# Filling matmuls between early pairs of first looks, and the grouped attention's first scores ahead of its last four value blocks

## The reference

```python
q = jnp.einsum('bsh,he->bse', x, w_q).reshape(b, sq, GROUPS, HPG, KVC)
k, v = jnp.split(jnp.einsum('bsh,he->bse', x, w_kv), 2, axis=-1)
scores = jnp.where(causal, jnp.einsum('bqgpd,bkgd->bgqpk', q, k) * SCALE, -jnp.inf)
ctx = jnp.einsum('bgqpk,bkgd->bqgpd', softmax(scores), v)
out = jnp.einsum('bse,eh->bsh', ctx, w_dense)
```

## Time and the profile before

| | us |
|---|---|
| median of three runs | 1053.94 |
| lowest, highest run | 1052.57, 1057.13 |
| the profiled execution | 1061.46 |
| its span in the trace | 1059.4 |
| TensorE busy in it | 972.7 (92%) |
| VectorE busy | 745.6 (70%) |
| ScalarE busy | 572.0 (54%) |
| GpSimd busy | 394.4 (37%) |

### The profile page before, as it was taken

The page is one execution under the profiler, slowest core; times in us unless marked ns, Lnnn a source line. Parts: engine busy times, 40 slices in busy tenths (PEclk is TensorE's granted clock), DMA queues, the critical chain, the costliest instruction groups (busy, mean ns, idle before and its releaser), DMA issues.

```text
span 1059.4 us, 20929 instructions
## 1 busy us (share of the span) xinstructions
PE 972.7 (92%) x7863; PEld 668.7 (63%) x7888; DVE 745.6 (70%) x1867; ACT 572.0 (54%) x1166; POOL 394.4 (37%) x259
## 2 busy tenths in 40 slices
PE   4999789999999999999988879999999999999897
PEld 3787633433443344688777657777777777777776
DVE  7856966888888883454666756777776777777655
ACT  6443413566666667544454545565655555565354
POOL 3010130045324540000244046565656555566254
PEclk9999978999999999999989999999999999999999
DMA  4020543255423502021010000000000000000001
GB/s 110 1 83 2 164 85 60 55 90 97 88 61 76 98 22 72 1 88 73 1 41 1 0 2 1 2 2 2 2 2 2 2 1 2 1 1 2 1 1 41
DMA packets 25373, 37.93 MB, mean 36 GB/s; under 512 B 3096, under 2 KB 21192, under 8 KB 23752
## 3 DMA queue, kind: packets, MB, share of 16 engines
q1 hardware_dynamic: 25272, 36.59, 14.6%
HBM read 30.53 MB, written 5.85 MB: 34 GB/s over the span
## 4 chain that ended last, share of the span: by engine, by line
PE 32%; DVE 8%; issue 5%; ACT 3%; POOL 2%; ACTq 0%; DVEq 0%; POOLq 0%
PE bank L1132 14%; PE pair L1572 7%; PE bank L1620 3%; PE bank L1608 3%; DVE mx L2007 3%; PE bank L1244 2%; POOL P L850 2%; ACT QH L858 1%; DVE xn L1732 1%; ACT P L1053 1%; PE bank L1162 1%; DVE hL L1790 1%; DVE stats L1722 1%; DVE CT L2049 0%; DVE hf L1784 0%
## 5 line engine op out<-in xcount | busy, mean ns | idle before, releaser
L850 POOL TENSOR_SCALAR P<-P,rec 128x1024 f32<-128x1024 f32 (+7 forms) x128 | 220.4, 1726 | 176.8 <-DVE rec L2032 176.8
L979 ACT ACTIVATE PT<-bank 128x512 f32<-128x512 f32 (+2 forms) x320 | 154.4, 559 | 109.0 <-PE bank L1383 90.8
L1870 DVE CUSTOM_DVE_ANT_0 bank<-bank,stripS 128x128 f32<-128x128 f32 (+1 forms) x224 | 129.9, 604 | 28.1 <-PE bank L1307 27.0
L1572 PE MATMUL pair<-KH,QH 128*128 128x512 f16 (+3 forms) x576 | 116.1, 329 | 16.4 <-ACT P L1053 13.8
L1053 ACT ACTIVATE P<-pair,nm 128x1024 f32<-128x1024 f32 (+7 forms) x128 | 95.5, 747 | 55.8 <-DVE nm L2011 55.7
L1620 PE MATMUL bank<-PT,VH 128*128 128x128 f16 x1728 | 117.2, 219 | 0.0
L1307 PE MATMUL bank<-KT,QT 96*128 96x512 bf16 (+2 forms) x336 | 103.0, 331 | 10.3 <-DVE MX L1870 8.4
L1620 PEld LDWEIGHTS bank<-PT,VH 128*128 128x128 f16 x1728 | 107.1, 98 | 2.7
L2040 DVE TENSOR_TENSOR PT<-bank,PT 128x384 f16<-128x384 f32 (+1 forms) x192 | 99.7, 547 | 11.3 <-ACT PT L858 11.3
L1784 DVE TENSOR_TENSOR hf<-sil,bank 128x512 f32<-128x512 f32 x64 | 43.9, 686 | 85.7 <-PE bank L1132 56.5
L2007 DVE TENSOR_REDUCE mx<-pair 128x1 f32<-128x1024 f32 (+7 forms) x128 | 95.7, 748 | 10.7 <-PE pair L1574 10.7
(11 more groups left out here) (188 smaller groups left out, 1942.5 us busy)
## 6 DMA issues: line engine op xcount, KB each, us to landing
KT<-qk_dram SPq DMA_DIRECT2D x21, 192.0 KB
stripS<-band_rows SPq DMA_DIRECT2D x28, 128.0 KB, 2.2
qk_dram<-parts SPq DMA_DIRECT2D x12, 256.0 KB, 2.2
stripT<-seq_dram SPq DMA_DIRECT2D x27, 88.0 KB, 8.7
q_raw<-w_gu SPq DMA_DIRECT2D x4, 512.0 KB, 10.7
w_raw<-w_dense SPq DMA_DIRECT2D x2, 1024.0 KB, 6.5
w_raw<-w_q SPq DMA_DIRECT2D x2, 1024.0 KB, 4.9
QT<-qk_dram SPq DMA_DIRECT2D x14, 128.0 KB
```

The costliest lines, as they stand in the source:

```text
L850: pool.tensor_scalar(rows, rows, rec1[:, m % 4:m % 4 + 1], None, ALU.mult).then_inc(s["pn"], 1)
L979: act.activation(PT[:, n % 4, hs[0]:hs[-1] + 1, 0:ni], src, ACT.Exp).then_inc(s["s2_exp"], 1)
L1572: ins = pe.matmul(out, QH1[:, h % 2, l, P * ib:P * (ib + 1)], KH1[:, r, h // (H1 // GR), HALF * c:HALF * c + nj], start=(i == 0), stop=(i ...
L1870: dve.tensor_tensor_reduce(out, out, stripS[:, h, HALF - nj:HALF], 1.0, LOWEST, ALU.add, ALU.max, mx).then_inc(s["s1_max"], 1)
```

## The change

1. Ten filling matmuls in `qkv`, into `pair[0]`, ahead of TensorE's wait for the second half of the normalised input.
2. Four filling matmuls into bank 5 behind each of pairs 9, 11 and 13.
3. Layer-1 weights 3 go from `grouped` into `ffn(2)` (t = 7 on ScalarE, t = 8 on VectorE); weights 4 follow block 8 and not block 10.
4. In `grouped`, only blocks 0 to 11 are made ahead of the loop, then both query blocks, then the first scores. Blocks 12 and 13 follow `scores(0)`, and 14 and 15 follow `scores(1)`. They go to banks 6 and 7. ScalarE takes their high parts on either side of the exponential of steps 0 and 1, VectorE takes their low parts behind the maximum of steps 0 and 1, and the wait for all low parts stands at the first product with values.

```diff
-        Q_FIRST = 14
+        KV_AHEAD = 12
         def kv_bank(t):
-            return bank[(4 if t < 8 else 0) + t % 4]
+            return bank[6 + t % 2] if t >= KV_AHEAD else bank[(4 if t < 8 else 0) + t % 4]
...
-        QUERY_WEIGHTS_AT = {8: 3, 10: 4}
+        QUERY_WEIGHTS_AT = {8: 4}
...
# ScalarE, grouped
+                def keys_high(t):
+                    act.wait_ge(s["k_mm"], t + 1)
+                    copy(kv_part(t, 0), kv_bank(t)).then_inc(s["k_hi"], 1)
...
+                    if n in (0, 1):
+                        keys_high(KV_AHEAD + 2 * n)
                     if 0 <= n < STEPS:
                         scores(n)
+                    if n in (0, 1):
+                        keys_high(KV_AHEAD + 2 * n + 1)
...
# ScalarE, beside ffn(2)
-                if t == 4:
-                    layer1_weights(2)
+                if t in (4, 7):
+                    layer1_weights(2 + t // 6)
...
# TensorE, qkv
                 norm_half(1, 1)
+                keep_clock(pair[0][:, 0:HALF], 10)
                 pe.wait_ge(s["ln_lo"], 4 * TR_OF_SUB[1] + 4)
...
# TensorE, attention
                 for n in range(8, EARLY_PAIRS):
                     look1_pair(n)
+                    if n % 2:
+                        keep_clock(bank[5], 4)
...
# TensorE, grouped: one block
+                    elif t >= KV_AHEAD + 2:
+                        pe.wait_ge(s["k_lo"], t - 1)
                     elif t not in range(8, 12):
                         pe.wait_ge(s["k_lo"], t - 3)
...
+                for t in range(KV_AHEAD):
...
+                    keys_values(t)
+                pe.wait_ge(s["k_lo"], 8)
+                pe.wait_ge(s["w1_lo"], 5)
+                for c in range(2):
+                    make_q(0, c)
+                pe.wait_ge(s["k_lo"], KV_AHEAD)
...
                     if n + 1 < STEPS:
                         scores(n + 1)
+                    if n < 1:
+                        for t in range(KV_AHEAD + 2 * (n + 1), KV_AHEAD + 2 * (n + 2)):
+                            keys_values(t)
...
                         m = n - PV_LAG
+                        if m == 0:
+                            pe.wait_ge(s["k_lo"], 16)
...
# VectorE, grouped
                     if 0 <= n < STEPS:
                         scores(n)
+                    if n in (0, 1):
+                        for t in range(KV_AHEAD + 2 * n, KV_AHEAD + 2 * n + 2):
+                            keys_low(t)
...
# VectorE, beside ffn(2)
-                if t == 5:
-                    layer1_weights(2)
+                if t in (5, 8):
+                    layer1_weights(2 + t // 7)
```

More of the change, by code:

```diff
@@ L1032, in grouped @@
             def grouped():
-                for t in range(16):
+                def keys_high(t):
+                    act.wait_ge(s["k_mm"], t + 1)
+                    copy(kv_part(t, 0), kv_bank(t)).then_inc(s["k_hi"], 1)
+                for t in range(KV_AHEAD):
                     if t == 1:
@@ L1037, in grouped @@
                         transposed(TR_OF_SUB[4], (1,))
[L1038 to L1042, removed]
+                    keys_high(t)
                     if t in QUERY_WEIGHTS_AT:
                         layer1_weights(QUERY_WEIGHTS_AT[t])
+                for c in range(2):
+                    queries_high(0, c)
                 def scores(n):
@@ L1532, in grouped, with keys_values @@
                 pe.wait_ge(s["w1_lo"], 3)
-                for t in range(16):
+                def keys_values(t):
                     kind, i = KV[t]
[L1535 to L1545, removed]
                     if t % 8 == 0:
@@ L1558, in grouped @@
                     ins.then_inc(s["k_mm"], 1)
-                pe.wait_ge(s["k_lo"], 16)
+                for t in range(KV_AHEAD):
+                    if t == 2:
+                        row_sums(2, 1)
+                    if t == 3:
+                        back(2, 1)
+                    if t == 7:
+                        norm_half(4, 1)
+                    keys_values(t)
+                pe.wait_ge(s["k_lo"], 8)
+                pe.wait_ge(s["w1_lo"], 5)
+                for c in range(2):
+                    make_q(0, c)
+                pe.wait_ge(s["k_lo"], KV_AHEAD)
                 def scores(n):
@@ L1983, in grouped, with keys_low @@
             def grouped():
-                for t in range(16):
+                def keys_low(t):
+                    dve.wait_ge(s["k_hi"], t + 1)
+                    dve.tensor_tensor(kv_part(t, 1), kv_bank(t), kv_part(t, 0), ALU.subtract).then_inc(s["k_lo"], 1)
+                for t in range(KV_AHEAD):
                     if t == 2:
@@ L1993, in grouped @@
                         transposed(TR_OF_SUB[4], (1,))
[L1994 to L1998, removed]
+                    keys_low(t)
                     if t in QUERY_WEIGHTS_AT:
                         layer1_weights(QUERY_WEIGHTS_AT[t])
+                for c in range(2):
+                    queries_low(0, c)
                 def scores(n):
```

## The result

The changed kernel is faster: the ratio to the kernel before is 0.9935, with a 95% interval from 0.9919 to 0.9951, from 20 runs of each. The medians are 1051.22 us (1049.18 to 1056.18) and 1058.87 us (1052.57 to 1064.64). The three runs of the kernel before that the prediction had, 1052.57 to 1057.13 us, belong to the lower part of its 20. The forecast was 1043.4 us with a range from 1040.5 to 1052. So the direction is right and the range holds the time, but the forecast is 7.8 us too low.

A forecast was written before the change was run, and what follows sets the result against it. TensorE was taken to bound the kernel nearly everywhere, with time to win where it waits or its clock is low. -7.8 + 0.8 - 4.0 = -11.0, less 0.5 given back, -10.5 from 1053.94: 1043.4 us, range 1040.5 to 1052.

The forecast's parts named there:

- The base: Whole kernel: the gain was subtracted from the runs' median, 1053.94 us, supposing the profile's extra 7.5 us lie elsewhere.
- The prediction's own sign: Whole kernel: the prediction is wrong if changed runs lie above 1049 us though the clock windows are at 1.00.
- Rival (a): First looks: the clock fall at 145 us isn't in the timed runs; time 1050.7 us, chance 0.20.
- part 2: Fills behind pairs 9, 11 and 13: clock stays at 2.4 GHz, last maximum at 161.0 us; gain 7.8 us.
- Part 1: Ten filling matmuls in qkv: 2.5 us fits in 3.50 us of TensorE idle time; costed at nothing, bounds 0 and +4.
- rival (d): Wait for V near 131 us grows to up to 2.9 us, clock falls; about +10, 1061 us, or +4; chance 0.04.
- Rival (b): First looks: the clock falls again behind pair 15, fills win only 3.3 us; time 1047.4 us, chance 0.13.
- Part 3: Layer-1 weights 3 moved into the second feed-forward: new TensorE stall of 0.8 us, bounds 0.3 and 3.5.
- Part 4: Grouped start: first scores 6.3 us sooner, GpSimd's start nearly unchanged, fifth scores sooner; gain 4.0 us.
- scores(4) start at 617.3: Grouped start: fifth scores begin at 617.3 us, after the first transposes, against 621.30 before.
- The sum: Whole kernel: -7.8 + 0.8 - 4.0 = -11.0 us, with 0.5 given back for handovers: -10.5.

The follow-up runs named there:

- pair_fill_at_9_only: The kernel before with one fill of four matmuls behind pair 9 only; median 1056.65 us, ratio 0.9984.
- queue_reordered: Changed kernel without qkv fill, with early ScalarE table load, VectorE's first reciprocal and step 2 maximum ahead of low parts; median 1046.41 us, ratio 0.9882.
- weights_not_moved: The changed kernel with layer-1 weights 3 and 4 left behind key blocks 8 and 10; median 1057.39 us, ratio 0.9995.

## Why the prediction was right or wrong, point by point

**The base was wrong, and this is the step that failed and cost most.** The prediction took the median of three runs and assumed "that the profile's 7.5 us lie elsewhere and not in the very stretch of half clock". They lay there for the most part. Two of the three runs, at 1052.57 and 1053.94 us, lie at the executions without the fall, and the profiled execution, at 1061.46 us, had it. In 80% of 92 executions, told by the mean clock, it is there, and the two groups' medians are 7.4 us apart (1060.3 against 1052.9). Subtracting a gain from a base that for the most part already had that gain gives a time that no run reached: 1043.4 where 1051.2 was measured. The prediction's own sign of this came: the windows are at 1.00 and all 20 runs lie above 1049 us. Rival (a) named it, with a chance of 0.20 and a time of 1050.7 us, which is close to the 1051.22 measured. It had the state of two of the three runs right, and was wrong to carry it over to the timed runs as a whole; that the stated range held the time is owed to rival (a), not to the forecast's sum. The Trainium skill's "TensorE: Matmul & The Clock Gate", section "What's actually happening", which the prediction set against itself, says that the number of slow matmuls at a kernel's start varies between runs of one kernel. It is the same for a fall in the middle of this kernel: the 92 executions are in two groups with a gap between them.

**A reading of the page that was wrong.** The row of granted clock in the earlier trace rows is below nine tenths in its sixth and seventh slices, 132 to 185 us, and again in the 21st, at 530 to 556 us, not in the fifth and sixth. The windows of the earlier trace rows, on which part 2 rests, were read rightly; the 21st slice holds the fall near 531 us that the sum left out.

**Part 1, costed at nothing, bounds 0 and +4.** In the median it is nothing that can be told (1050.54 against 1050.53). In the traces it did what rival (d) says in its mild form: TensorE ahead, a longer wait for V, clock down, 1.5 us at the first maxima. The clock was full again by 136 us, so the severe form, half clock up to 166 us, didn't come. A long fall at that place does exist: in the trace of pair_fill_at_9_only, which has no fill in qkv, it lasts from 130 to 144 us. The rival also held that the outcome is decided near 2.5 us of idle time, from one wait of 2.52 us with half clock behind it and one of 2.45 with full. The length doesn't decide it: the same wait of 2.52 us left the clock at full in two other traces.

**Part 2, -7.8 us.** The mechanism was right. In the trace it was 7.2; the laid-out order was 0.7 us too fast at its end. In the median it was 5.7; one execution in five had no fall to cure. (The busy time around the first two fills, put at 1.4 and 3.4 of 3.8 us, is 1.55 and 3.55 by the earlier trace rows; the sum doesn't use it.) Rival (b), a second fall behind pair 15, is in none of the nine traces with three fills of four; one of the changed kernel's 20 executions, 1056.18 us at a mean clock of 0.987, may have had such a one.

**Part 3, +0.8 us.** It was 0.0. The step that failed was to price this piece partly by the sister piece: that one ran 3.38 us, this one 2.28, at the lower bound, and the 0.3 us of stall reckoned from 2.29 us didn't appear in TensorE's timeline either.

**Part 4, -4.0 us.** It was 2.9. The order of events was as forecast up to GpSimd's first step (21.4 us behind key block 8 forecast, 21.6 measured), table load on the chain included. The step that failed is "scores(4) start at 617.3": I had let the maximum of step 2 follow scores(2) at once. In VectorE's queue the low part of head 1's first queries stands ahead of it, and waits for TensorE's make_q and ScalarE's copy, so the maximum began at 608.84 us though its scores were done at 606. TensorE then waited 0.85 us more for that exponential. queue_reordered takes this, the reciprocal's place and the table load away, and wins 3.45 us on that distance. And the base was one execution here too: 1.4 of the 2.9 us are the half clock at the third scores, which two of the five traces with the old start don't have.

**The sum.** -10.5 us forecast, -10.0 in the traced spans, of which 1.5 us are a fall at 531 us that one profiled execution had and the other had not. So the traced sum agrees partly by chance: without it, it is -8.5, and without the fall at the third scores -7.1. For the median I can only give a rough sum, since medians of two kinds of execution don't add: part 2 at the frequency of the fall is 0.80 x 7.2 = 5.8 us, and part 4 is 1.4 to 2.9, together 7.2 to 8.7 us. The medians differ by 7.65.

## What to carry to other kernels

Before subtracting a gain from a median, find out whether the executions behind the median have the loss: a cluster of times with a cluster of mean clocks says so, and three runs don't. When work moves to the front of an in-order queue, walk through every queue up to the next steady state, not only up to the first engine that catches up: one low part ahead of one maximum cost 0.85 of the forecast 4.0 us here. And where several short waits follow each other and the clock falls, small fills in all of them (three of two matmuls) did more here than one larger fill in the first (four).

## What the runs showed of the hardware

The granted clock of the same instructions with the same waits fell in 74 of 92 executions and not in 18. It is not settled by the idle time alone: waits of 1.19 and 1.08 us left it at full in one execution, and waits of 1.18 and 1.08 us at half in another, a wait of 2.52 us left it at full in two traces and at half in three, and one of 0.85 us at full in five and at half in three. After a fall here, at 145 us, TensorE was busy nearly without a break for 20 us before the clock came back; behind the fall at 115 us, with the projections running, it was back in 3 us, though in two other traces in about 7. The falls after which TensorE ran the feed-forward (at 531 us), the queries (weights_not_moved) or the scores of the grouped attention cost 1.4 to 1.6 us each, the one among the first looks 7. Three fills of two matmuls, some 0.5 us each, were enough to prevent it in 11 of 12 executions.
